# Moving block-maxima units between quads of an attention and mixture-of-experts kernel

## The reference

```python
x = x + layernorm(attention(layernorm(x)))     # 16 heads of 16, blocks of 64, sparse pattern
x = x + layernorm(ffn(layernorm(x)))           # 8 experts, top 2, rotations by expm, a gate
```

## Time and profile before

| what | value |
|---|---|
| time, median of 3 runs | 1752.6 us (1749.86 to 1754.69) |
| profiled execution | 1753.1 us |
| span of the trace | 1751.3 us |
| PE busy | 1516.0 us (87%) |
| DVE busy | 1223.2 us (70%) |
| ACT busy | 896.1 us (51%) |
| POOL busy | 696.6 us (40%) |
| mean granted TensorE clock | 0.965 |

### The profile page before, as it was taken

How to read it: one execution, slowest core, us unless ns; L and a number is a source line. 1 busy time by engine, 2 the same in 40 slices (tenths; PEclk the granted TensorE clock), 3 DMA queues, 4 the chain that set the end, 5 groups by cost and what they waited for, 6 DMA issues and landing times. The chain is left out here.

```text
span 1751.3 us, 33300 instructions
## 1 busy us (share of the span) xinstructions
PE 1516.0 (87%) x10277; PEld 1049.1 (60%) x10342; DVE 1223.2 (70%) x3687; ACT 896.1 (51%) x1782; POOL 696.6 (40%) x705
## 2 busy tenths in 40 slices
PE   7889889989988998999899898799999999999500
PEld 5655455545545554555455466688888888888400
DVE  5667787888788787878877846356555656565287
ACT  3146766776676667667666664233333333333244
POOL 1011233533442443245334325144444444444468
PEclk9999999999999999999999999899999999999855
DMA  8132244345435533543554338656565665655397
GB/s 230 42 109 81 87 151 152 118 134 171 134 105 168 164 113 120 176 140 105 161 161 119 104 131 262 159 104 139 113 137 120 132 121 129 124 123 98 47 330 236
DMA packets 186076, 243.04 MB, mean 139 GB/s; under 512 B 23576, under 2 KB 156576, under 8 KB 185824
## 3 DMA queue, kind: packets, MB, share of 16 engines
q1 hardware_dynamic: 159360, 205.40, 37.3%
q0 software_dynamic: 26592, 36.07, 12.4%
HBM read 133.12 MB, written 105.64 MB: 136 GB/s over the span
## 5 line engine op out<-in xcount | busy, mean ns | idle before, releaser
L1112 ACT ACTIVATE pexp<-scT 128x512 f32<-128x512 f32 x768 | 433.4, 598 | 254.3 <-PE scT L868 222.6
L1317 DVE TENSOR_REDUCE mx<-work 128x1 f32<-128x320 f32 (+2 forms) x1024 | 500.3, 546 | 62.2 <-PE work L841 61.5
L1882 POOL DMA_INDIRECT y_rows<-rows_add,row_of x142 | 225.5, 1588 | 292.0 <-DMA y_rows<-rows_add,row_of 229.7
L841 PE MATMUL work<-w 126*128 126x320 bf16 (+4 forms) x1280 | 269.3, 295 | 30.4 <-DVE mx L1317 27.3
L868 PE MATMUL scT<-w 128*128 128x192 bf16 (+3 forms) x1472 | 261.5, 270 | 35.1 <-ACT pexp L1112 30.6
L1914 PE MATMUL h_ps<-inT,w1c 128*128 128x256 f32 x1136 | 259.5, 382 | 2.4 <-DVE inT L1966 2.4
L1927 PE MATMUL o_ps<-w,hT 128*128 x1136 | 256.8, 379 | 0.0
L1857 ACT ACTIVATE rows_add<-rows_out,row_share 128x257 f32<-128x257 f32 x142 | 64.6, 503 | 350.5 <-DVE rows_out L1982 301.3
L1914 PEld LDWEIGHTS h_ps<-inT,w1c 128*128 128x128 f32 x1136 | 217.3, 192 | 33.1 <-issue 3.3
L868 PEld LDWEIGHTS scT<-w 128*128 128x128 bf16 x1536 | 123.3, 97 | 173.5 <-ACT pexp L1112 126.9
L1927 PEld LDWEIGHTS o_ps<-w,hT 128*128 128x128 f32 x1136 | 210.5, 190 | 25.8
(11 more groups left out here) (204 smaller groups left out, 2065.6 us busy)
## 6 DMA issues: line engine op xcount, KB each, us to landing
w<-split_spill SPq DMA_DIRECT2D x384, 128.0 KB, 2.9
split_spill<-split SPq DMA_DIRECT2D x64, 384.0 KB, 3.1
rows_in<-z_rows SPq DMA_DIRECT2D x71, 265.0 KB, 4.8
y_rows<-pre SPq DMA_DIRECT2D x16, 514.0 KB, 5.6
y<-y_rows SPq DMA_DIRECT2D x16, 514.0 KB, 6.8
x_rows<-x SPq DMA_DIRECT2D x16, 512.0 KB, 2.8
abel_rows<-pre SPq DMA_DIRECT2D x16, 512.0 KB, 3.7
abel_in<-abel_rows SPq DMA_DIRECT2D x16, 512.0 KB, 4.6
```

Source lines behind the costliest of these rows:

```text
L841: ins = nc.tensor.matmul(out[:, at:at + hi - lo], tile(qst[par][0:K_SCORE, h, :], t), kst[par][0:K_SCORE, h, lo:hi], start=True, stop=True)
L1112: nc.scalar.activation(pexp[:, (q * GROUP + n) % NPB, :], scT[n % 2][:, :], ACT.Exp, scale=DH ** -0.5).then_inc(s_exp, 1)
L1317: emptied(nc.vector.reduce_max(mx[:, c:c + 1], bank(s, "max", b, h, t)[:, 0:n], AX_X), s, "max", b, h, t)
L1882: pool.indirect_dma_start(kept.y_rows, bass.IndirectOffsetOnAxis(ap=row_of[n][:, r:r + 1], axis=0), rows_add[n % 2][:, r, :], None, comput ...
```

## The change

Three edits, all in `front`:

1. `LATE_AT`: the late units of the own step's quad 11 go from four (one at n = 1, one at n = 2, two at n = 3) to two (both at n = 3). The head of the next step takes six instead of four: three behind projection 0, one behind each other.
2. `fill`: the 48 early units are spread over 26 places, n = 1 to 3 of quads 3 to 11 without the last one (11, 3), instead of two in each of the 24 places of quads 3 to 10.
3. VectorE's order: the maxima of ("proj", 0) come before parts(0) rather than behind it.

The text of `order_of` is the same; its sequence follows from the first two.

```diff
-LATE_AT = [("end", 1), ("end", 2), ("end", 3), ("end", 3),
-           ("proj", 0), ("proj", 1), ("proj", 2), ("proj", 3),
+LATE_AT = [("end", 3), ("end", 3), ("proj", 0), ("proj", 0), ("proj", 0),
+           ("proj", 1), ("proj", 2), ("proj", 3),
            ("quad", 0, 3), ("quad", 0, 3), ("quad", 1, 3), ("quad", 1, 3), ("quad", 1, 3),
            ("quad", 2, 1), ("quad", 2, 2), ("quad", 2, 3)]
...
             units = [(h, t) for h in range(EARLY) for t in range(NT)]
-            span = QUADS - 1 - B_FROM
-            if not B_FROM <= q < QUADS - 1:
+            places = [(q_, n_) for q_ in range(B_FROM, QUADS) for n_ in range(1, GROUP)][:-1]
+            if (q, n) not in places:
                 return []
-            some = units[(q - B_FROM) * len(units) // span:(q - B_FROM + 1) * len(units) // span]
-            third = -(-len(some) // 3)
-            return some[(n - 1) * third:n * third]
+            i = places.index((q, n))
+            return units[i * len(units) // len(places):(i + 1) * len(units) // len(places)]
...
+                behind("proj", 0)
                 for m in range(4):
 
                     if proj:
                         parts(s, m)
                     if finish and m % 2:
                         finish_a(s - 2, m // 2)
-                    behind("proj", m)
+                    if m:
+                        behind("proj", m)
```

## The result

The changed kernel takes 1805.6 us (median of 5 runs, 1801.0 to 1808.0) against 1751.7 us (5 runs, 1749.9 to 1754.7). The ratio is 1.031, 95% interval 1.029 to 1.033. That is 54 us slower, where 31 us were forecast with an upper end of 1800. The direction was right and the time lies outside the range. The profiled execution took 1801.0 us, the shortest of the five; its span is 1799.2 us.

What follows compares the result with a forecast made beforehand. TensorE was taken to bound the kernel, working 54.8 us of each 60.6 us step. From a median of 1752.6 us, 23 us for twelve steps, 8.5 us for starts 1 to 3 and -0.5 us gave +31 us: 1783 us, range 1768 to 1800.

Steps and rivals of the forecast that it cites:

- Point 3: Head of the next step: project 1 takes project 0's bank and waits for its emptying; 2.37 us later for all that follows.
- the rival of the clock: TensorE's gap before project 1 lets the clock fall; 2.5 us in each of twelve steps, 30 us, 1813 us; chance 0.12.
- The sum: +1.9 us in each of steps 4 to 15, 23 us; starts 1 to 3 8.5 us; last step -0.5 us; together +31 us.
- Point 1: Quads 3, 5, 7 and 9: one unit fewer each ahead of quad 11; gain of 1.3 us per step, 0.5 to 1.9.
- Point 2: Quad 11: turn_max waits for a unit's reduction, 1.2 us later; next project(0) 0.8 us later per step.
- The starts without gelu: Starts 1 to 3: project 1 +2.5 us, quad 11 +0.8 us, less a smaller gain; 3.2 + 2.9 + 2.4 = 8.5 us.
- The end: After the attention part: experts and output come later by the same and don't change; the last step takes -0.5 us.
- The rival on the other side: Head: part 0's bank is emptied before TensorE finishes three units, so the wait is hidden; -7 us, 1745 us; chance 0.05.

Runs made afterwards that it cites:

- e1: Changed kernel with 16 transposes of unused result on TensorE between the three units behind projection 0 and projection 1; 1786.6 us, ratio 1.021.
- e2: Changed kernel with the six late units of the head dealt 1, 2, 2, 1 behind projections 0 to 3; 1765.2 us, ratio 1.008.
- e3: Kernel before with the new late-unit list and VectorE's new order, early units still dealt over eight quads; 1798.4 us, ratio 1.028.
- e8: Kernel before, one early unit each moved from (3,1) and (9,2) to (11,1), five late head units dealt 1, 1, 2, 1; 1754.9 us, ratio 1.001.
- e4: Kernel before with VectorE's new order alone; 1750.3 us, ratio 1.000.
- e9: Kernel before with only the early units dealt over nine quads; 1751.4 us, ratio 1.001.
- e10: Kernel before with the early units of e8, five late head units dealt 2, 1, 1, 1, and VectorE's new order; 1739.6 us, ratio 0.994.
- e11: Kernel before with the early units of e8, head and VectorE's order as before, quad 11's late unit at n = 1 moved to n = 2; 1739.5 us, ratio 0.994.
- e6: Changed kernel with 8 transposes of the identity in the wait before projection 1; 1788.4 us, ratio 1.021.
- e7: Changed kernel with 4 transposes of the identity in the wait before projection 1; 1804.6 us, ratio 1.030.

## Why the prediction was right and wrong

**Point 3, the head, was right, in mechanism and in size.** 2.37 us were worked out from the earlier trace rows; without the fall of the clock it is 2.30 us (e1 against before), in 2.38 us of waiting. In starts 1 to 3 the head grew by 2.4 us, where 2.5 us were worked out. e2 and e3 show it from both sides: the banks apart, the loss goes; the late units alone, it stays.

**The step that failed is the rival of the clock.** The sum took the clock as staying up and gave its fall a chance of 0.12, because the gap to come, 2.4 us, lay between one of 1.76 us that had left the clock up and one of 3.18 us that had not the earlier trace rows. That was an open question, and it was closed by taking the kinder answer. In the profiled execution it fell in nine of the twelve starts 4 to 15. Its price was 1.69 us for a fall, where I had 2.5 us, so 15 us rather than 30 us: 1783 + 15 = 1798 us, against 1801 us for the profiled execution. The other four executions took 1804.6 to 1808.0 us at mean granted clocks of 0.954 to 0.957, against 0.958 in the profiled one. That fits more falls in them, but it isn't shown: no trace of them was kept. With the range reaching only to "some starts with a fallen clock", 1800, it left out the true median by 6 us. The page "TensorE: Matmul & The Clock Gate" of the Trainium skill, section Part 1: The HAM clock gate, has the clock fall to half after idling. The runs here agree that the gap is the cause of the slow projections: 1786.6 us with it filled, 1805.6 us without.

**Point 1, the gain of thinner quads, was nearly right.** Forecast 1.3 us ahead of quad 11. From the first value projection to the transposes of quad 10 it is 1.16 us (before 627.18 less 584.99, after 656.68 less 615.65). Of these 0.80 us are won by the transposes of quad 8 (before 618.93, after 648.79) and 0.36 us in quads 8 and 9, where 0.7 and 0.6 us had been worked out. e8 gets 1.13 us with two units moved in place of four (627.20 less 586.14): 0.52 us by quad 8 (619.56) and 0.61 us in quads 8 and 9. So thinning quads 5 and 7 brought 0.28 us ahead of quad 8, and quad 9 took it back: its one wait is 1.14 us in the changed kernel and 0.96 us in e8.

**Point 2, quad 11, was right in kind and a little small.** turn_max waits for the reduction as forecast (0.95 us), but it starts 0.32 us after the last reduction ends (599.31 to 599.63 in the changed kernel), where the working had 0.08 us. turn_max came 1.4 us later instead of 1.2 us, and the next projection 0 by 1.1 us instead of 0.8 us. Together with point 1 the stretch from the first value projection to the next projection 0 should have won 0.5 us and won 0.06 us. This makes 62.84 us for a step with the clock up, where the sum had 60.6 + 1.9 = 62.5 us: about 0.3 us more in each of twelve steps.

**The starts without gelu.** The three waits before project 1 are 1.90, 1.83 and 1.83 us, and the clock stayed up. By turn_max of step 3 the kernel was 11.2 us behind (280.27 against 269.05), against 8.5 us for the starts and some gains in the working. Step 1 alone took 57.06 us instead of 51.69 us, 5.4 us more where 3.2 us had been worked out; another 0.95 us were lost by turn_max of step 0 (103.27 against 102.32), ahead of the starts that the sum counts. In step 1 TensorE waits for the stacks of that batch, which come by DMA. In quad 3 (timelines of PE: before, changed, e3, e4):

```profile
124.58 0.53 PE L841 MATMUL work<-w 126*128 126x320 bf16 x2 [0.76 <-DMA w<-split_spill]
```

```profile
128.54 0.45 PE L840 MATMUL work<-w 126*128 126x320 bf16 x1 [2.01 <-DMA w<-split_spill]
```

```profile
125.39 0.53 PE L841 MATMUL work<-w 126*128 126x320 bf16 x2 [0.42 <-DMA w<-split_spill]
```

```profile
125.26 0.87 PE L841 MATMUL work<-w 126*128 126x320 bf16 x2 [2.20 <-DMA w<-split_spill]
```

In the changed kernel the clock fell behind this wait (0.60 from 128 to 130, 0.54 from 130 to 132). But the traces don't show that the change made it longer. e3 has the late wait for project 1 and waits 0.42 us here; e4 has none and waits 2.20 us, with a fall of the clock as well (0.57 in the mean from 124 to 132), and its step 1 took 55.65 us. So between the profiled executions of these kernels this wait differs by nearly 2 us, for a reason that the runs leave open. What the forecast left out is that the wait exists at all.

**The end.** At the last turn_max the changed kernel was 52.5 us behind (1048.03 against 995.56), at the end of the span 47.9 us. The last step stands 2.81 us at its start instead of 3.18 us, and the clock was below 1.00 there from 1053 to 1057 instead of from 999 to 1007 (0.57 in the mean of either stretch). The rest was not traced; the same stretch to the end took 751 us in the changed kernel, e3 and e9 and 753 to 757 us in the other runs, so it is about the scatter of that part. Added up for the profiled execution: 31 us forecast, 15 us of falls in starts 4 to 15, 3 us more in starts 0 to 3, about 3 us of step length and 4 us less at the end make the 48 us by which its span is longer.

**The rival on the other side** (the bank wait hidden, 1745 us) had its condition named rightly: parts(0) would have had to end 2.4 us earlier, and no kernel here did that. What wins is not to hide the wait but not to have it: e10 and e11.

## What to carry to other kernels

When instructions share buffers in rotation, moving work between stages also moves who waits for whom: write down, for the new order, which item each one inherits its buffer from, and price that wait first. Move work away from the places where the bounding engine waits, not evenly: two units taken from two waits won as much ahead of quad 10 as four dealt evenly (1.13 and 1.16 us), and the four had to be paid for behind it (11 us won in e10 and e11, nothing in e9). When a change makes TensorE stand for a new gap whose effect on the clock the trace leaves open, price both answers and let the range hold both.

## What the runs showed of the hardware

- Four transposes more or less in a gap decided on 16 us of the kernel (e6 1788.4 us, e7 1804.6 us). In the profiled executions, standing 1.50 us before project 1 (e6) left TensorE's granted clock at 2.4 GHz in all of the starts 4 to 15; standing 1.93 us (e7) or 2.38 us (the change) was followed by some us at 1.2 GHz in nine of them, and each cost 1.69 us. The same kernel had starts of both kinds at the same gap, 62.8 and 64.5 us long.
- None of these lengths is safe or sure by itself: the clock fell after 1.58 us in step 1 of e1 and after 1.85 us in step 0 of e6, and it stayed after 1.85 and 1.90 us in steps 0 and 1 of the changed kernel.
- Transposes whose results nobody uses, into a bank that is free, can hold the clock: 1786.6 us with 16 of them in each gap, 1788.4 us with 8, 1804.6 us with 4, 1805.6 us with none.
- A transpose that waits for VectorE's last reduction (turn_max) started 0.32 us after that reduction ended; a unit that waits for its bank started 0.06 us after it (603.79 by the earlier trace rows, where the first reduction takes 0.48 us from 603.25).
